# Layernorm, causal attention and a 32-expert layer in one kernel: positions and the transposes of the expert stage moved

## What is computed

```
xn = layernorm(x)
qkv = xn @ W_qkv ; scores = q k^T / 16, causal ; attn = softmax(scores) @ v       # 8 batches of 2048
shared = (silu(xn @ sg) * (xn @ su)) @ sd
logits = xn @ gate_w                      # 32 experts, 256 -> 512 -> 256
e = argmax(logits), s = sigmoid(max(logits))
order = argsort(e) ; y = (xn * s)[order]
d = (silu(y @ rg[e]) * (y @ ru[e])) @ rd[e]     # each row with the weights of its own expert
x + attn + shared + d[inverse of order]
```

## Time and profile before

| | us |
|---|---|
| runs: median, lowest, highest (3) | 2384.75, 2382.6, 2385.98 |
| the profiled execution: its own time | 2384.18 |
| its span, first to last instruction | 2382.2 |
| PE busy | 2316.4 (97%) |
| DVE, ACT, POOL busy | 1565.0, 1216.2, 1065.6 |
| mean granted TensorE clock | 0.992 of full speed |

### The profile page before, as it was taken

The page is one execution under the profiler, slowest core; times in us unless marked ns, Lnnn a source line. Parts: engine busy times, 40 slices in busy tenths (PEclk is TensorE's granted clock), DMA queues, the critical chain, the costliest instruction groups (busy, mean ns, idle before and its releaser), DMA issues. The chain is left out here.

```text
span 2382.2 us, 48635 instructions
## 1 busy us (share of the span) xinstructions
PE 2316.4 (97%) x16118; PEld 2136.5 (90%) x16118; DVE 1565.0 (66%) x3322; ACT 1216.2 (51%) x2254; POOL 1065.6 (45%) x1031
## 2 busy tenths in 40 slices
PE   7999999999978999999999997999999999999998
PEld 6888888888868999999999995898988888888888
DVE  6777777777757777777777774646455555555555
ACT  3344434444425556656655653555555555555545
POOL 2333332333323333333333330666666666666667
PEclk9999999999998999999999999999999999999999
DMA  6665566665556766776767776334343444434331
GB/s 221 217 213 200 205 219 226 213 209 204 203 190 218 239 231 235 243 235 229 243 233 230 243 239 233 103 100 134 117 138 119 132 127 128 139 120 161 123 114 51
DMA packets 301977, 439.23 MB, mean 184 GB/s; under 512 B 35968, under 2 KB 209792, under 8 KB 301824
## 3 DMA queue, kind: packets, MB, share of 16 engines
q1 hardware_dynamic: 283712, 398.90, 48.9%
q0 software_dynamic: 18112, 38.37, 6.0%
HBM read 288.21 MB, written 148.96 MB: 184 GB/s over the span
## 5 line engine op out<-in xcount | busy, mean ns | idle before, releaser
L1231 POOL TENSOR_TENSOR t_p_lo<-t_score,t_p_hi 128x512 fp32r<-128x512 f32 (+1 forms) x320 | 360.0, 1131 | 190.7 <-ACT t_score L1355 113.9
L884 POOL DMA_INDIRECT ahead_rows<-xs_rows,ahead_slot x160 | 182.7, 1142 | 417.8 <-DMA ahead_slot<-token_of 257.7
L1347 ACT COPY t_score<-t_psS 128x512 f32<-128x512 f32 (+1 forms) x320 | 167.5, 523 | 332.5 <-PE t_psS L71 229.7
L1428 PE MATMUL t_psO<-t_v_hi,t_p_hi 128*128 128x258 f32 x1088 | 318.3, 293 | 0.9 <-DVE t_outb L1309 0.9
L1430 PE MATMUL t_psO<-t_v_hi,t_p_lo 128*128 128x258 f32 x1088 | 307.6, 283 | 0.0
L1432 PE MATMUL t_psO<-t_v_lo,t_p_hi 128*128 128x256 f32 x1088 | 306.6, 282 | 0.0
L1285 DVE TENSOR_TENSOR t_top<-t_top,t_psS 128x512 f32<-128x512 f32 (+3 forms) x264 | 155.1, 587 | 167.6 <-ACT t_score L1347 163.0
L305 POOL DMA_INDIRECT token_of<-a_token_i,a_slot_i x128 | 141.6, 1107 | 242.9 <-DVE a_slot_i L415 213.7
L69 PE MATMUL t_psS<-t_q_hi,ahead_x_hi 128*128 128x512 f32 (+3 forms) x640 | 233.8, 365 | 6.5 <-DVE t_q_lo L1267 5.5
L71 PE MATMUL t_psS<-t_q_lo,ahead_x_hi 128*128 128x512 f32 (+3 forms) x640 | 233.6, 365 | 0.0
L70 PE MATMUL t_psS<-t_q_hi,ahead_x_lo 128*128 128x512 f32 (+3 forms) x640 | 232.9, 364 | 0.0
(11 more groups left out here) (187 smaller groups left out, 7334.9 us busy)
## 6 DMA issues: line engine op xcount, KB each, us to landing
ahead_raw<-in_L_ffn_routed_gate_w SPq DMA_DIRECT2D x42, 512.0 KB
ahead_raw<-in_L_ffn_routed_up_w SPq DMA_DIRECT2D x42, 512.0 KB
ahead_raw<-in_L_ffn_routed_down_w SPq DMA_DIRECT2D x41, 512.0 KB, 5.0
e_raw<-in_L_ffn_routed_gate_w SPq DMA_DIRECT2D x41, 512.0 KB
e_raw<-in_L_ffn_routed_up_w SPq DMA_DIRECT2D x41, 512.0 KB
e_raw<-in_L_ffn_routed_down_w SPq DMA_DIRECT2D x41, 512.0 KB, 4.8
routed_rows<-e_dout SPq DMA_DIRECT2D x80, 256.0 KB, 4.4
a_xt<-in_L_attn_x SPq DMA_DIRECT2D x32, 512.0 KB, 5.9
```

What stands on the lines that cost most here:

```text
L884: g.indirect_dma_start(out=xg[:, k, h], out_offset=None, in_=xs, in_offset=bass.IndirectOffsetOnAxis(slot[:, k, h:h + 1], 0)).then_inc(x_i ...
L1231: g_.tensor_tensor(p_lo[:, t % LR, c0:], score[:, t % SR, c0:], p_hi[:, t % HR, c0:].bitcast(F32), ALU.subtract).then_inc(lo_ok, 1)
L1347: s.copy(score[:, t % SR, c0:], psS[:, n % BANKS, c0:]).then_inc(u_act, 1)
L1428: nc.tensor.matmul(psO[:, a, 0:W], p_hi[:, kp, cols], v_hi[:, kv, j % J], start=j == 0, stop=False, skip_group_check=True)
```

## The change

Two edits. The positions: the product and the reduction move from the attention stage into the first four tiles of the expert stage on DVE, two pairs in each tile, into buffers of their own (`moved`, `begin`), and the sum comes at the end of DVE's expert stream. POOL in the attention stage no longer waits for them, nor does ACT for the score buffer. The transposes: PE makes `transposes(t+1)` between q = 0 and q = 1 of `up(t)`, not after it; ACT makes `x_high(t+1)` after the silu of q = 0, ahead of the high part of the up weights; DVE makes `x_low(t+1)` after `mul(t, 0)`, ahead of `low(t+1, 1)`. SP's and POOL's streams of the expert stage are as before.

```diff
@@ expert_stage
+        NT = keep.rank.shape[1]
+        TP = NT // 8
+        moved = sb("moved", [P, TP, E])
+        begin = sb("begin", [P, NT])
+        pos_step = sem("pos_step")
@@ expert_stage, vector
+            def positions(m):
+                ts = slice(m * TP, (m + 1) * TP)
+                wait(dve, pos_step, 2 * m)
+                v.tensor_tensor(moved[:], keep.one_hot[:, ts], keep.shift[:].unsqueeze(1).to_broadcast([P, TP, E]),
+                                ALU.mult).then_inc(pos_step, 1)
+                wait(dve, pos_step, 2 * m + 1)
+                v.tensor_reduce(begin[:, ts], moved[:], AX.X, ALU.add).then_inc(pos_step, 1)
+
             def step(t, k, i):
                 low(t + 1, 1 - k, 0)
                 mul(t, 0)
+                x_low(t + 1, 1 - k)
                 low(t + 1, 1 - k, 1)
                 h_low(t, k, 0)
                 mul(t, 1)
                 low_down(t, k)
-                x_low(t + 1, 1 - k)
+                if isinstance(t, int):
+                    positions(2 * t)
                 h_low(t, k, 1)
+                if isinstance(t, int):
+                    positions(2 * t + 1)
             tiles(dve, step)
+            dve.wait_ge(pos_step, 16)
+            v.tensor_tensor(keep.position[:], begin[:], keep.rank[:], ALU.add)
@@ expert_stage, scalar
             def step(t, k, i):
                 high(t + 1, 1 - k, i + k, 0)
                 silu_of(t, 0)
+                x_high(t + 1, 1 - k)
                 high(t + 1, 1 - k, i + k, 1)
                 h_high(t, k, 0)
                 silu_of(t, 1)
                 h_high(t, k, 1)
-                x_high(t + 1, 1 - k)
@@ expert_stage, tensor
-            def up(t, k):
+            def up(t, k, i):
                 wait(pe, xl_ok, t + 1)
                 for q in range(Q):
+                    if q == 1:
+                        transposes(t + 1, 1 - k, i + k)
...
             def step(t, k, i):
-                up(t, k)
-                transposes(t + 1, 1 - k, i + k)
+                up(t, k, i)
                 if not is_first(t):
                     down(t - 1, 1 - k)
@@ attention_stage, gpsimd
-            pool.wait_ge(pos_ok, 1)
             gather(0)
             gather(1)
@@ attention_stage, vector
-            def positions(m):
...
-            def position_sum():
...
-                if 2 <= step < 2 * NP + 2:
-                    positions(step - 2)
-                elif step == 2 * NP + 2:
-                    position_sum()
@@ attention_stage, scalar, keep_score
-                if t == SR - 2:
-                    act.wait_ge(pos_ok, 1)
```

More of the change, by code:

```diff
@@ L1132, in attention_stage @@
         negmax = sb("negmax", [P, J])
[L1133 to L1136, removed]
         spread = sb("spread", [P, J, P], F32R)
@@ L1159, in attention_stage @@
         base_ok = sem("base_ok")
-        pos_step, pos_ok = sem("pos_step"), sem("pos_ok")
         block = st.enter_context(nc.Block())
@@ L1249, in _ @@
             v = nc.vector
-            def positions(m):
[L1252 to L1258, removed]
-            def position_sum():
-                dve.wait_ge(pos_step, 2 * NP)
-                v.tensor_tensor(keep.position[:], start, keep.rank[:], ALU.add).then_inc(pos_ok, 1)
             def q_low(g, c):
```

## The result

The changed kernel takes 2552.81 us (median of 4 runs, 2551.12 to 2554.68), the kernel before 2385.36 beside it (2382.6 to 2387.49, 4 runs): a ratio of 1.0703, 95% interval 1.0684 to 1.0721. It is 167 us slower where 79 were forecast, and above the range (2408 to 2530).

A forecast was written before the change was run, and what follows sets the result against it. PE, busy 97% of the span, was taken as the bound. 2384.18 + 77 (steady loop) + 2 (start) + 0 (positions) = 2463, the median 0.6 higher: 2464 us; range 2408 to 2530, the forecast's own 2425 to 2500.

The forecast's parts named there:

- The first term: Steady expert loop: rows wanted 2.80 us earlier against 1.65 us spare, 1.15 us short in the mean tile, 45 us.
- the growth of L in part 1: Steady expert loop: rows' lateness grows beyond 1.15 us as weight loads come nearer; 0.8 us taken, giving 77 us.
- bound of 1.6: Steady expert loop: most the rows' lateness could grow, 0.4 us of SP lateness plus 1.2 us of nearer weights; 109 us.
- two-step rule: Steady expert loop: rows count from two steps back, so two steps together lose the rows' lateness, each step half.
- index lists asked for later than S + 2.3: Expert steps: sign of being right, SP asking for lists later than 2.3 us after the start of `up(t)`.
- The Trainium skill's rule on semaphore writes: Gathers' release in the expert loop: nearer weights also delay it; by this alone the sum is 109 us.
- Rival (a): Expert loop: stops lower PE's clock, 39 stops costing 1.6 us each, 62 us more, 2526 us; chance 0.16.
- (b): Expert loop: rows come in time after a few steps, a fourth of the sum stays, 2405 us; chance 0.10.
- (c): Rows land within 2.9 us of the second gather, PE never stops, faster at 2379 us; chance 0.06.
- (d): No change: rows in time at times, the win at the start is spent, 2385 us; chance 0.05.
- The start: First expert steps: `up(1)` near 727.1, then a stop of some 5 us for tile 2's rows until 735.2; net +2 us.
- The positions: Moved DVE work: -1 us in the attention stage, +1 in four expert steps, together 0.

The follow-up runs named there:

- e8: e3 with the x splits moved right behind the second weight split: 2420.96 us, ratio 1.014.
- e3: Kernel before with only PE's transposes moved to mid step, x splits and positions unmoved: 2433.39 us, ratio 1.0205.
- e10: e7 with the positions left in the attention stage: 2376.47 us, ratio 0.9966.
- e11: e8 with one wait more: SP issues the gate and up weights only after `h_low(t, 0)`: 2523.33 us, ratio 1.0588.
- e9: e2 with only half of the experts' weights loaded in the loop, same instructions and waits, output not right: 2434.88 us, ratio 1.0199.
- e7: Changed kernel with tile t+3's index list asked for in step t ahead of the up weights, tile 2's first of all: 2382.45 us, ratio 0.9991.
- e12: Kernel before with transposes and x split in mid step in step 0 only, positions unmoved, index lists as before: 2382.54 us, ratio 0.9997.
- e1: Kernel before with only the positions moved into the expert stage: 2389.27 us, ratio 1.002.
- e2: Kernel before with only the transposes and x splits moved to mid step, positions unmoved: 2551.04 us, ratio 1.0692.

## Why the prediction was wrong in size

**Sign and mechanism held.** PE stops at its transposes for the gathered rows, 60 listed waits and 123.8 us, and PE busy is 93%: both as foretold, though a stop is 2.1 us and not some 1 us, and a step 11.1 and not 9.9. The first term, 2.80 us earlier demand against 1.65 us spare, held roughly. Over steps 6 to 76 of the kernel before the last packet ends 1.97 us ahead of the transposes, less 0.4 for the release: 1.57 us spare. 45 us were forecast with nothing moved behind it, and 36 measured in e8, whose rows land 0.6 us earlier than before, which the sum did not have. The 49 of e3 are closer by luck: some 16 of them are the wait for `x_low`.

**The step that failed is the growth of L in part 1**, "I take 0.8 us, the middle", with a bound of 1.6. Rows landed at S + 12.54 before and at S + 15.01 after: 2.5 us later. By the two-step rule a step is half of (landing + 0.4 release + 6.0 for what is left of up and down behind the transposes):

| | step by the rule | x 79 |
|---|---|---|
| landing of before (12.54) | 9.47, less 8.96 | 40 us |
| landing later by 2.47 | 1.24 | 98 us |
| remainder to 11.12 | 0.42 | 33 us |

Together 171 us, the growth of the stage. Landing times are those of steps 6 to 77, the step is that of all 79, so some 7 us of the remainder belong to steps outside of these, the start above all (on 6 to 77 alone the remainder is 0.33 us a step). The bound of 1.6 counted how much nearer the loads come when nothing stops (1.2 us; e10, with no stops, has the gate load 1.3 us later than before) plus SP's own lateness. What it left out is a loop: `low(t+1, 1)` now stands behind `x_low`, and `x_low` behind a stop of PE, so each stop puts the gate load off further (S + 8.85, not 7.1), onto the index list and both gathers. Of the 2.5 us, list to first gather takes 0.8 (3.62 before, 4.43 after), the second gather's start to its last packet 1.3 (4.57 and 5.88). My sum drew the loads up to the list from the front; it did not ask what happens when they run beside the gathers. e11 (one wait, 102 us) and e9 (half the bytes, back by 116) show both sides of it.

**A sign was wrong on the way:** "index lists asked for later than S + 2.3" as the thing to look for. They are asked for at the same place (2.98 and 2.86); list and rows only land later. What did come true is that `load_down` falls right ahead of the next store: on the mean 0.70 us, before 1.33. It puts off the landing of the list and not the asking: from issue to landing the list takes 3.66 us, before 2.85.

**The Trainium skill's rule on semaphore writes** was cited for the upper bound. Releases came about 0.4 us behind the last packet in the kernel after, as in the 0.45 us of the earlier trace rows; what grew was the time to the last packet. By the Trainium skill ("DMA: Bandwidth & Descriptors", Queues, rings and completion order) the semaphore write waits for earlier writes of its engine; the trace shows no growth behind the last packet that this would have to explain, and can't exclude it inside the gather.

**Rival (a), 0.16, came true in part.** Half clock is in 26 stretches in the expert stage, most of 3.4 us, before in 2, nearly all at stops of 1.8 us or more. What it costs can be read off the path. From a tile's transposes to the end of the step in which they stand it takes 6.60 us on the mean of steps 6 to 76, in e10 6.08; in those 6.60 the clock is half for 1.02 us, which costs 0.51. By the two-step rule that is 0.26 us a step, about 20 us in 79. The rest of the 33 is the 7 us above and what the rule leaves out, above all tiles that were in time: by the same rule e9 keeps a remainder of 0.47 us a step with 3 stretches of half clock. No run removed the clock's fall alone. The forecast of 62 for it was too much, and the whole still went beyond it, because L was the larger miss. Rivals (b), (c) and (d) did not come: with the lists ahead (e7) (d) is what the whole change would do.

**The start held.** Timeline of PE after:

```profile
726.94 0.28 PE L69 MATMUL e_psG<-e_x_hi,e_whi 128*128 128x256 f32 x1
...
735.53 1.12 PE L1011 MATMUL e_psT<-keep_ident,ahead_rows 128*128 128x128 f32 x4 [5.63 <-DMA ahead_rows<-xs_rows,ahead_slot]
736.65 0.41 PE L70 MATMUL e_psG<-e_x_hi,e_wlo 128*128 128x256 f32 x1
```

`up(1)` at 726.94 (727.1 forecast) and a stop of 5.63 us until 735.53 (735.2). But the granted clock is half from 734.0 to 740.8, so 5.3 us of work behind the stop lose 2.6, where I allowed 1.6 at most: `up(2)` begins at 744.06, against 740.1 before, +4 where +2 was forecast. e12 does not have these 4 us, since only tile 1's transposes are moved there: PE has q = 1 to do before it needs the rows of tile 2, `up(2)` begins at 740.8, and the time is that of before. So no run shows the start of the changed kernel by itself.

**The positions were mis-sized:** 0 forecast, +4.5 (e1) measured. The -1 in the attention stage is 0 (930.9 us against 930.8), and the +1 is 3.3 (by the traces) to 4.5: the cover named, `h_low` and `mul` "needed only in the next step", isn't there where DVE already has little room and four such tiles stand in a row.

## What to carry to other kernels

A wait that the profile does not show has a margin: before a consumer is moved forward, measure how long before it its data land, and then ask which bulk loads the move sends onto that data, above all where the load's issue hangs on the consumer itself, since then every stop makes the next one longer. A small transfer that a step hangs on belongs ahead of the megabytes in the queue, a step early if its buffer allows: here one line's place in SP's stream, with a first call ahead of the loop, turned 7% slower (e2) into 0.3% faster (e10). Price the move from the time at which each transfer lands, not only from the order of issue.

## What was not expected of the hardware

**The same gather on POOL lasts 0.94 to 2.0 us.** Durations (ns min/median/max) of all 160 gathers, before, after, e9, e11 and e10:

```profile
L884 POOL DMA_INDIRECT ahead_rows<-xs_rows,ahead_slot x160: 941/998/1963, 727.6 to 1435.2; - x160
```
```profile
L889 POOL DMA_INDIRECT ahead_rows<-xs_rows,ahead_slot x160: 940/1434/2008, 727.4 to 1604.4; - x160
```
```profile
L886 POOL DMA_INDIRECT ahead_rows<-xs_rows,ahead_slot x160: 943/1418/2009, 726.2 to 1480.6; - x160
```
```profile
L886 POOL DMA_INDIRECT ahead_rows<-xs_rows,ahead_slot x160: 940/966/1987, 726.2 to 1566.6; - x160
```
```profile
L885 POOL DMA_INDIRECT ahead_rows<-xs_rows,ahead_slot x160: 940/969/1227, 720.8 to 1425.5; - x160
```

The gather of 2.00 us above (1207.37 to 1209.37) ran beside the last two of these on DVE, subtractions of two SBUF tiles:

```profile
1206.14 0.68 DVE L928 TENSOR_TENSOR e_h_lo<-e_h,e_h_hi 128x512 fp32r<-128x512 f32 x1
...
1207.34 1.22 DVE L914 TENSOR_TENSOR e_wlo<-e_raw,e_whi 128x1024 fp32r<-128x1024 f32 x1
1208.48 0.69 DVE L928 TENSOR_TENSOR e_h_lo<-e_h,e_h_hi 128x512 fp32r<-128x512 f32 x1
```

Of the 160 in the kernel after, 51 last about 2.0 us, and such subtractions (`low`, `low_down`, `h_low`) cover on the mean 0.89 of their time; 25 last under 0.97 us, with 0.12 covered. The Trainium skill ("GPSIMD Engine Reference", 1. Specifications) says that GpSimd's SBUF interfaces are shared with VectorE, with contention where a DVE instruction has two SBUF inputs; the trace of the kernel after goes with it. That DVE is the cause is not shown: in e9 29 gathers last under 0.97 us although the same work covers 0.82 of their time, so the overlap alone does not decide it. It is not where most of the time went: e9 has gathers as long as the kernel after (1418 and 1434 ns) and loses 50 us and not 167, e11 has short ones (966) and loses 139.

**When a load is issued can cost more than how much is loaded.** Between e8 and e11 the bytes are the same and 1 MB a step is issued 2.0 us later; that is 102 us.

**Half the clock behind stops of PE.** The forecast had a stop of 2.21 us that was followed by half the clock and one of 1.46 us that was not the earlier trace rows. The kernel after has some 60 stops. Each of the 25 stretches of half clock that begin in its steps begins during a stop of 1.84 us or more or within 1.5 us behind it; none of its 15 shorter stops had one. But 20 stops of 1.85 to 2.49 us had none either, and in e11 one of 3.20 us had none, so the length of a stop alone doesn't decide it. In e8, where 30 of 33 stops last under 1.3 us, the mean clock of the expert steps is 1.00.
